# Products over 64 rows in 32-column tiles for C·state and the Gram matrix of an SSD chunk scan

## The reference, cut to what matters

```python
def ssd_chunk_scan(X, dA, Bm, Cm, chunk):
    # X: (b,l,h,p); Bm, Cm: (b,l,g,n), repeated over the heads of a group
    A_cum = jnp.cumsum(A, axis=-1)
    Lm = jnp.exp(segsum(A))
    Y_diag = jnp.einsum('bcshn,bczhn,bhcsz,bczhp->bcshp', Cm, Bm, Lm, X)
    states = jnp.einsum('bcshn,bhcs,bcshp->bchpn', Bm, decay_states, X)
    ...
    Y_off = jnp.einsum('bcshn,bchpn,bhcs->bcshp', Cm, states, state_decay_out)
    return (Y_diag + Y_off).reshape(b, l, h, p)
```

## Time and profile before

| What | Value |
|---|---|
| median of 3 runs | 792.37 us (790.32 to 793.12) |
| the profiled execution's own time | 786.84 us |
| its span, first to last instruction | 785.0 us |
| mean granted TensorE clock | 0.947 of full |
| TensorE matmul busy | 685.0 us (87%) |
| VectorE busy | 530.8 us (68%) |
| ScalarE busy | 368.4 us (47%) |
| GpSimd busy | 377.4 us (48%) |
| prologue, first matmul of `main_part` at | 118.08 us |
| `main_part`'s units with a burst | 139.5 to 607 us |

### The profile page before, as it was taken

One profiled execution on the slowest core, in us unless ns is written; L12 is line 12 of the kernel. 1 busy time (PEld: TensorE's weight loads), 2 busy tenths in 40 slices (PEclk: granted clock), 3 DMA queues, 4 the chain that ended last, 5 costly groups with the idle time before them and its releaser, 6 DMA issues. The chain is left out here.

```text
span 785.0 us, 20689 instructions
## 1 busy us (share of the span) xinstructions
PE 685.0 (87%) x8200; PEld 531.6 (68%) x8200; DVE 530.8 (68%) x933; ACT 368.4 (47%) x779; POOL 377.4 (48%) x453
## 2 busy tenths in 40 slices
PE   6677348999989999989999989999988568899994
PEld 6456116777767777767777767877766256688883
DVE  2759576878757777767777758787865515666663
ACT  0562413455544644555644554645444214565653
POOL 2674800144635535445435446345343048676771
PEclk9997578999999999999999999999999769999998
DMA  7341352111132022132022033122025543344411
GB/s 196 108 161 28 134 182 64 34 59 62 70 89 75 32 87 88 34 122 78 33 88 87 32 95 105 34 78 70 33 90 215 171 130 105 94 133 126 144 40 42
DMA packets 61333, 71.55 MB, mean 91 GB/s; under 512 B 13928, under 2 KB 32872, under 8 KB 61236
## 3 DMA queue, kind: packets, MB, share of 16 engines
q1 hardware_dynamic: 54500, 67.81, 26.8%
q10 hardware_dynamic: 6736, 2.41, 1.3%
HBM read 54.45 MB, written 15.75 MB: 89 GB/s over the span
## 5 line engine op out<-in xcount | busy, mean ns | idle before, releaser
L1149 DVE SCALAR_TENSOR_TENSOR m_cv<-bank,gpc,m_cv 128x511 f32<-128x511 f32 (+2 forms) x192 | 143.5, 748 | 50.0 <-ACT m_cv L1061 45.4
L903 PE MATMUL bank<-h_hi,w_hi 128*128 128x512 f32 x384 | 159.0, 414 | 12.6 <-DVE m_Xp L1235 11.5
L903 PE MATMUL bank<-h_hi,w_lo 128*128 128x512 f32 x384 | 151.4, 394 | 0.0
L903 PE MATMUL bank<-h_lo,w_hi 128*128 128x512 f32 x384 | 151.4, 394 | 0.0
L1061 ACT ACTIVATE m_cv<-bank,gpc 128x512 f32<-128x512 f32 x96 | 71.7, 747 | 103.2 <-PE bank L903 103.2
L1292 POOL TENSOR_TENSOR m_S<-m_S,m_cd 128x128 f32<-128x128 f32 x96 | 39.7, 414 | 140.2 <-DVE m_S L1212 70.3
L1597 PE MATMUL bank<-h_hi,t_y_hi 128*128 128x512 f32 x256 | 85.4, 406 | 14.6 <-POOL t_y_lo L1502 14.6
L903 PEld LDWEIGHTS bank<-h_hi,w_hi 128*128 128x128 f32 x384 | 73.1, 190 | 33.2 <-DVE m_Xp L1235 11.7
L1283 POOL TENSOR_TENSOR m_Xw<-m_Xp,wend 128x256 f32<-128x256 f32 x64 | 39.8, 621 | 114.4 <-ACT m_Xp L1081 114.4
L903 PEld LDWEIGHTS bank<-h_hi,w_lo 128*128 128x128 f32 x384 | 72.5, 189 | 17.0
L903 PEld LDWEIGHTS bank<-h_lo,w_hi 128*128 128x128 f32 x384 | 73.0, 190 | 13.6
(11 more groups left out here) (176 smaller groups left out, 1315.9 us busy)
## 6 DMA issues: line engine op xcount, KB each, us to landing
m_ea<-ea_scratch SPq DMA_DIRECT2D x32, 256.0 KB
m_dd<-dd_scratch SPq DMA_DIRECT2D x32, 256.0 KB
y_scratch<-m_t SPq DMA_DIRECT2D x16, 512.0 KB, 3.3
h_lo_place<-y_scratch SPq DMA_DIRECT2D x16, 512.0 KB, 4.2
p_wm<-in_L_wmod_dram SPq DMA_DIRECT2D x6, 1024.0 KB, 6.4
m_wraw<-in_L_attn_in_proj_w_dram SPq DMA_DIRECT2D x18, 256.0 KB, 3.5
p_xt<-in_L_attn_input__dram SPq DMA_DIRECT2D x16, 256.0 KB, 2.8
w_lo_place<-in_L_attn_input__dram SPq DMA_DIRECT2D x16, 256.0 KB, 4.5
```

What stands on the lines that cost most here:

```text
L903: ins = pe.matmul(A[k % 3][:, :], w[:, t, kc, :], h[:, n % NB, kc, :], start=(m == 0), stop=(m == 11))
L1149: ins = dve.scalar_tensor_tensor(out=cv[:, k % 3, lag:], in0=A[k % 3][:, 0:L - lag], scalar=s.gpc[:, gp, o:o + 1], in1=cv[:, k % 3, lag:], ...
```

## The change

`Ct` becomes `[P, 2, L]` without the zero halves and without its memset, and one instruction of 128 rows writes it. `offdiagonal` uses 64 rows and 32 columns per weight load with 64 columns moved: 8 products per chunk in place of 1. Its results of group q go to bank q of `YS`. `gram` becomes 8 products over 64 rows with 64 columns moved, in place of 4 over 128 rows with 128, and writes to columns 384 to 447 of the two banks of `YS` in place of `GB`. The transposed B moves to columns 0 to 127 of `GB`. `turn_b` no longer waits for `mix`; `offdiagonal` does. VectorE's `collect` and `update` now wait for the Gram product that ends the burst too.

```diff
-        Ct = sb("Ct", [P, 2, 2, L])
+        Ct = sb("Ct", [P, 2, L])
...
-                wait(pe, m_done, 2 * u)
                 wait(pe, bt_read, u)
-                pe.transpose(GB[:, P:2 * P], Bt[:, n % 2, tok(u)], s.ident[:, :]).then_inc(bt_done, 1)
+                pe.transpose(GB[:, 0:P], Bt[:, n % 2, tok(u)], s.ident[:, :]).then_inc(bt_done, 1)
...
             def offdiagonal(u):
...
                 pe.wait_ge(s_new, n_new(u, 1))
+                pe.wait_ge(m_done, 2 * u + 2)
                 for c in range(2):
                     if u % UPS == 0 and c == 0:
                         continue
-                    ins = pe.matmul(YS[:, c, P:2 * P], S[:, (2 * u + c - 1) % 4, :], Ct[:, n % 2, :, chunk(u, c)],
-                                    start=True, stop=True)
+                    for j in range(4):
+                        for q in range(2):
+                            group, strip = slice(64 * q, 64 * q + 64), slice(32 * j, 32 * j + 32)
+                            ins = pe.matmul(YS[strip, q, P + Q * c:P + Q * c + Q], S[group, (2 * u + c - 1) % 4, strip],
+                                            Ct[group, n % 2, chunk(u, c)], start=True, stop=True)
...
             def gram(u):
...
-                    ins = pe.matmul(GB[32 * m:32 * m + 32, 0:P], Bt[:, n % 2, first:first + 32], Ct[:, n % 2, :, chunk(u, m // 2)],
-                                    start=True, stop=True)
+                    for q in range(2):
+                        group = slice(64 * q, 64 * q + 64)
+                        ins = pe.matmul(YS[32 * m:32 * m + 32, q, 384:384 + Q], Bt[group, n % 2, first:first + 32],
+                                        Ct[group, n % 2, chunk(u, m // 2)], start=True, stop=True)
...
-                act.activation(BTs[:, :], GB[:, P:2 * P], ACT.Copy).then_inc(bt_read, 1)
+                act.activation(BTs[:, :], GB[:, 0:P], ACT.Copy).then_inc(bt_read, 1)
...
-                if t == 3:
-                    for q in range(2):
-                        rows = slice(64 * q, 64 * q + 64)
-                        ins = dve.scalar_tensor_tensor(out=Ct[rows, n % 2, q, :], in0=A[k % 3][rows, :], scalar=1.0,
-                                                       in1=cv[rows, k % 3, :], op0=ALU.add, op1=ALU.mult)
-                    ins.then_inc(silu_done, 1)
-                    return
-                dst = (xs[:, n % 2, 0, :], xs[:, n % 2, 1, :], Bt[:, n % 2, :], None, gate[:, 0, :], gate[:, 1, :])[t]
+                dst = (xs[:, n % 2, 0, :], xs[:, n % 2, 1, :], Bt[:, n % 2, :], Ct[:, n % 2, :], gate[:, 0, :], gate[:, 1, :])[t]
...
-                g = GB[:, q * Q:(q + 1) * Q].unsqueeze(1).broadcast_to([P, HG, Q])
+                g = YS[:, q, 384:384 + Q].unsqueeze(1).broadcast_to([P, HG, Q])
...
             def collect(u):
...
+                dve.wait_ge(g_done, min(u + 2, NU))
...
-                own, off = (YS[:, :, k * P:(k + 1) * P].rearrange("p c (q s) -> p c q s", q=2) for k in range(2))
+                own = YS[:, :, 0:P].rearrange("p c (q s) -> p c q s", q=2)
+                off = YS[:, :, P:2 * P].rearrange("p q (c s) -> p c q s", c=2)
...
             def update(u, c):
...
                 wait(dve, yd_done, u)
+                dve.wait_ge(g_done, u + 1)
...
-            dve.memset(Ct[:, :, :, :], 0.0)
             dve.memset(Xp[:, :, :, :], 0.0).then_inc(zeroed, 1)
```

## The result

| | before | after |
|---|---|---|
| median of 20 runs each, us | 789.8 (784.9 to 794.2) | 797.9 (791.2 to 802.5) |
| ratio, 95% interval | | 1.0104 [1.0086, 1.0122] |
| profiled execution / span, us | 786.8 / 785.0 | 797.9 / 796.2 |
| mean granted clock in it | 0.947 | 0.923 |

What follows compares the result with a forecast made beforehand. TensorE's own work was taken to bound the kernel. 63 bursts at -0.17 us gave -10.7, +2.0 given back, -0.4 and -1.4: -10.5 from 792.4, so 782 us; its range 776.5 to 788, with slower bound 790.5.

Steps and rivals of the forecast that it cites:

- part 2: Products with the state: 32 records for 4, hidden under the copy of B, 0; about -0.4 us in six bursts.
- part 1: Gram in diagonal's tile shape: the pause ahead of it goes, 16 records at 11 ns each, -0.17 us a burst.
- Rival B: Pauses around gram aren't from the change of tile shape, so they stay: about 791 us, chance 0.11.
- Part 3: Wait for mix moved from turn_b to offdiagonal: counted 0, up to 0.3 us back in one burst.
- part 4: VectorE's silu 0.69 us a step shorter, its update and collect wait for gram: 0, at worst +1.7 us.
- Part 5: Start, without the memset of Ct: first projection 1.92 us sooner, worth -1.4 us.
- Given back: Savings lost in 12 bursts ahead of TensorE's waits for raw weights and Xw, behind GpSimd and SyncE: +2.0 us.
- Rival A: At steps' first units GpSimd's queue binds in all 16 steps, 5.4 us lost instead of 2.0: 785 us, chance 0.12.
- Rival C: Issue price per small matmul, 22 ns each, makes offdiagonal 0.70 us and states late: 801 us, chance 0.09.
- The clock: TensorE's stretches at the lower clock behind waits: 1 to 2 us each, one more or less within the range.

Runs made afterwards that it cites:

- the products with the state alone: Kernel before with only the products with the state cut into 64-row, 32-column tiles, gram as before: 794.3 us, ratio 1.0063.
- gram only: Kernel before with only gram's new tiles in YS and the waits that belong to it, C and products with the state as before: 785.8 us against 789.6, ratio 0.9932.

## Why the prediction was wrong

**The step that failed is part 2's zero**, with the pitch of part 1 that it rests on: 11 ns a record, taken from diagonal, priced the added products by the pitch at which TensorE starts them and by nothing else. The price was right and even too high: by the row

```profile
L944 PE MATMUL pair<-m_Ct,m_S 64*32 64x64 f32 x1792 | 27.9, 227 | 1.5 <-DVE m_M L1183 1.5
```

and the burst above, 32 records start in 0.46 - 0.227 = 0.23 us, 7.5 ns each. They hide under the copy of B, states stands at +0.73. But each also costs two instructions, a load and a product, out of a supply that I never counted, though the page has a line for it: 66 packets in 785 us, one in 7 us in the main part, is a resource like the others, and a burst of 184 instructions in 2.15 us already used it at several times its mean pace. The change takes a burst to 256 in 1.95 us. What the runs showed in place of the zero: 19 pauses, 20.4 us, for late instructions in the change's trace, nine pauses, 9.7 us, in that of the products with the state alone, and a kernel 8.1 us slower. What it should have been weighed against, an engine that is faster than its supply for one burst, was nowhere in the sum, and no end of the range held it.

- **Part 1, gram.** Right in kind, mis-sized a little: -0.20 us a burst where -0.17 was summed, and the pause ahead of gram is gone. Rival B (791) falls with it.
- **Part 3, the moved wait, and part 4, VectorE.** TensorE waits for mix twice, 1.5 us, where 0 was counted for both parts and 0.6 us once stood. The chain that part 4 described is there behind the burst of unit 59: VectorE's copy of the state waits for gram, mix is queued behind it, and the burst of unit 60 waits 0.90 us for mix.

```profile
592.14 0.29 DVE L1213 COPY m_S<-pair 128x128 f32<-128x128 f32 x1 [0.75 <-PE pair L984]
```

In all, VectorE stood still ahead of its updates for 9.7 us in 11 waits for diagonal in the kernel before, and for 29.4 us in 23 waits for gram after the change. Little of it reached TensorE.
- **Part 5, the start.** TensorE waits 9.4 us for VectorE in place of 11.5, as forecast. The first projection stands at 114.6, not at 116.2:

```profile
113.66 0.91 DVE L1235 MEMSET m_Xp<- 128x1024 f32 x1 [2.54 <-PEq L134]
...
114.62 0.80 PE L903 MATMUL bank<-h_hi,w_hi 128*128 128x512 f32 x1 [9.36 <-DVE m_Xp L1235]
```

About 1.5 us more came from a memset that began earlier (113.66, where the first began at 115.19). That is mostly the spread of the prologue and not the change: GpSimd's first memset, which the change leaves alone, began at 113.37 in place of 114.69, 1.3 us earlier. The edit's own gain at the start, counted from that memset to the first projection, is 2.1 us (1.25 in place of 3.39), where 1.92 was forecast.
- **Given back.** Too small. 2.0 us were summed, and in gram only the waits for weights grew by 1.9. But the stretch gained only 6.8 us there and 10.7 where those waits are gone, so with the clock behind them 3.9 us came back. Rival A, more of it at Xw in all steps, isn't seen.
- **Rival C** had the sign and about the time (801), and not the mechanism: it asked for states being late behind a 0.70 us offdiagonal, which is 0.46 us long.
- **The clock** was left within the range as "one stretch more or less". In the stretch TensorE was at the lower level for 23.9 us after and 6.8 before. Of the 23.9, 10.2 stand at the three waits for raw weights, as in gram only. The other 13.7 begin at 580.9 and 594.5 us, in the units 57 to 60, where pauses at borders follow each other and waits for ScalarE stand between them; behind the pauses in the units 3 and 15 to 51 that stand apart from such waits the clock stayed at the full level. Against the kernel before it is up to 8.5 us more, since half of the time at half speed is lost; part of it lies in the pauses themselves.

The account of the stretch: 61 x -0.20 = -12.2, + 20.7 in pauses at borders, which makes + 8.5; 14.0 were measured. The other 5.5 lie within what the clock can cost, with 0.9 more for mix. This split of the last 5.5 was not measured by itself. In the medians the whole change costs 8.1 us, less than in the two traces, since the traced execution of the kernel before is 3.0 us below its median. The forecast of 782 us counted down from 792.4, the median of three runs; from the 789.8 of 20 runs the same gain of 10.5 would have given 779.3.

**What stays open.** The pace of supply isn't settled. The shortest distance between two borders is 3.36 us: the next packet starts 0.97 us behind a border and its block is usable 2.39 us later (the row at 304.08). But other packets started 2.5 to 2.9 us behind their border or later, the one of the block at 166.81 among them, and I found no rule for when one is asked for. In a profile of any one execution, only some of the bursts that could pause do so.

## What to carry to other kernels

When a change swaps one large product for many small ones, count the instructions as well as their time: weight loads and semaphore instructions count, fp32 products count twice (two loads and two matmuls in the records), and what matters is how long 256 in a row last, not the mean. In the four kernels here with the small products with the state, 33 blocks in the main part were through in less than 4.2 us; 26 of them ended in a pause, of 0.4 to 1.9 us, all eleven that took under 3.3 us among them. After such a pause expect more in the next blocks, even where these last 5 us or longer. A wait "<- issue" in the middle of a group of products, at places that have nothing in common but their number, is the mark of it, and a few idle instructions put in ahead show it within one run, because the pauses move.

## What the runs showed of the hardware

- **Instruction supply.** Pauses of up to 2.0 us, 12 of the 20 over 1.1 us, on TensorE at borders of 256 instructions, 19 of them ending 2.3 to 2.7 us behind the start of a 16 KB packet. They move when 96 instructions are put in ahead. The Trainium skill (Runtime: NRT & Kernel Launch, Instruction fetch mechanics) says that instructions are refilled in 16 KiB blocks of 256 while the block before runs, and that crossing a boundary is "mostly hidden". The traces agree with the size of the block. The trace of the kernel before agrees with "hidden": all its blocks in the main part last 6.3 us or more. The trace after does not, where a burst goes through a block in under about 4 us and in up to three blocks behind that.
- **Small products side by side** start 7.5 ns apart over 32 records (L944) and 11 over 64. The Trainium skill (TensorE: Matmul & The Clock Gate, Wait — 56ns, not 53.3ns?) has a floor of about 25 ns from start to start; these two rows lie below it.
- **A change of tile shape** costs 0.15 to 0.19 us at a group's edge, and keeping one shape from states to gram gives back 0.20 us a burst, over the main stretch 10.7 us where nothing gave it back. Gram changed its bank along with its shape. That a change of bank alone costs this is unlikely: from turn_b to the products with the state the bank changed before too, and they started 0.11 us apart; after the change, where the shape changes there as well, it is 0.20.
